# A second buffer for copied sums, a new order on VectorE, and the differences of xin stored in pairs

## The reference

```python
def _L0_cond_ref(x, c, weight, c_weight, bias):
    ...
    out = lax.conv_general_dilated(x, weight, window_strides=(STRIDE,), padding=[(PAD, PAD)], dimension_numbers=('NCH', 'OIH', 'NCH'), feature_group_count=GROUPS)
    ctx = jnp.einsum('nd,od->no', c, c_weight)
    out = out + ctx[:, :, None] + bias[None, :, None]
    return out

def _L1_cond_ref(x, embedding, W0, b0, W1, b1, W2, b2, weight, bias_k):
    ...
    att = jax.nn.softmax((h @ W2 + b2) / T, axis=-1)
    agg_w = jnp.einsum('bk,koi->boi', att, weight[..., 0])
    agg_b = att @ bias_k
    out = jnp.einsum('boi,bih->boh', agg_w, x) + agg_b[:, :, None]
    return out
...
x = x + _L0_cond_ref(x, cond_128, L0_cond_weight, L0_cond_c_weight, fside_S_0)
x = x + _L1_cond_ref(x, cond_128, L1_cond_W0, ...)
x = x + _L2_cond_ref(x, cond_128, L2_cond_weight, L2_cond_c_weight, fside_S_0)
x = x + _L3_cond_ref(x, cond_128, L3_cond_W0, ...)
```

## Time and profile before

| | us |
|---|---|
| median of 3 runs | 2769.24 (2769.07 to 2769.81) |
| the profiled execution's time | 2770.05 |
| its span in the trace | 2768.2 |
| TensorE matmul busy | 2622.8 (95%) |
| VectorE busy | 2150.6 (78%) |
| ScalarE busy | 1492.8 (54%) |

### The profile page before, as it was taken

How to read it: one execution, slowest core, us unless ns; L and a number is a source line. 1 busy time by engine, 2 the same in 40 slices (tenths; PEclk the granted TensorE clock), 3 DMA queues, 4 the chain that set the end, 5 groups by cost and what they waited for, 6 DMA issues and landing times.

```text
span 2768.2 us, 57051 instructions
## 1 busy us (share of the span) xinstructions
PE 2622.8 (95%) x24812; PEld 1174.4 (42%) x24812; DVE 2150.6 (78%) x815; ACT 1492.8 (54%) x852; POOL 36.7 (1%) x31
## 2 busy tenths in 40 slices
PE   6699999999999999999999999999999999999998
PEld 3244444444444444444444444444444444444443
DVE  4578788788788787787887887887887887878873
ACT  2345555555555555555555555555555555555554
POOL 5000000000000000000000000000000000000000
PEclk8699999999999999999999999999999999999999
DMA  5634434334334334334334334334434444443433
GB/s 155 212 131 142 122 114 146 119 114 150 115 114 152 114 114 152 114 114 152 114 115 150 114 121 144 121 121 136 129 121 129 132 126 122 139 123 117 144 92 107
DMA packets 185494, 357.06 MB, mean 129 GB/s; under 512 B 12715, under 2 KB 143795, under 8 KB 152635
## 3 DMA queue, kind: packets, MB, share of 16 engines
q1 hardware_dynamic: 184576, 352.37, 40.6%
q10 hardware_dynamic: 898, 4.39, 0.6%
HBM read 205.72 MB, written 150.99 MB: 129 GB/s over the span
## 4 chain that ended last, share of the span: by engine, by line
PE 66%; DVE 23%; issue 5%; ACT 5%; DMA 2%; DVEq 0%; ACTq 0%; SPq 0%
PE psum L313 25%; PE psum L325 22%; PE psum L350 17%; DVE diff L546 17%; DVE y L602 5%; ACT y L475 4%; DMA mix_dram<-y 1%; DVEq L137 0%; DVE y L595 0%; ACT y L464 0%; DMA select_sb<-select 0%; PE psum L274 0%; PE psum L303 0%; DMA mixw<-mix_dram 0%; ACT x L515 0%
## 5 line engine op out<-in xcount | busy, mean ns | idle before, releaser
L313 PE MATMUL psum<-diff,prod_w 32*128 32x512 f32 x8192 | 932.1, 596 | 89.0 <-DVE diff L546 69.6
L546 DVE TENSOR_TENSOR diff<-xin 128x2052 f32<-128x2052 f32 x256 | 984.4, 3890 | 0.0
L350 PE MATMUL psum<-y,mixw 32*128 32x512 f32 x8192 | 917.2, 595 | 20.2 <-DMA mixw<-mix_dram 13.7
L325 PE MATMUL psum<-diff,prod_w 32*128 32x512 f32 (+1 forms) x8192 | 773.2, 600 | 0.0
L472 ACT COPY shared<-psum 128x2048 f32<-128x2048 f32 x256 | 477.8, 1866 | 493.8 <-PE psum L313 493.8
L602 DVE TENSOR_TENSOR y<-y,shared 128x2048 f32<-128x2048 f32 x128 | 293.4, 2292 | 542.5 <-ACT y L475 542.5
L313 PEld LDWEIGHTS psum<-diff,prod_w 32*128 32x128 f32 x8192 | 414.9, 185 | 594.6 <-issue 410.6
L350 PEld LDWEIGHTS psum<-y,mixw 32*128 32x128 f32 x8192 | 418.5, 186 | 503.3 <-issue 497.6
L475 ACT COPY y<-psum 128x2048 f32<-128x2048 f32 x256 | 477.8, 1867 | 273.0 <-PE psum L325 273.0
L546 DVE TENSOR_TENSOR diff<-x 128x2055 f32<-128x2055 f32 x256 | 576.5, 2295 | 9.6 <-ACT x L515 9.6
L325 PEld LDWEIGHTS psum<-diff,prod_w 32*128 32x128 f32 (+1 forms) x8192 | 314.4, 158 | 435.8 <-issue 419.2
(11 more groups left out here) (57 smaller groups left out, 91.7 us busy)
## 6 DMA issues: line engine op xcount, KB each, us to landing
xin<-x SPq DMA_DIRECT2D x128, 1024.0 KB, 6.6
out<-outb SPq DMA_DIRECT2D x128, 1024.0 KB, 4.7
mixw<-mix_dram SPq DMA_DIRECT2D x512, 128.0 KB, 5.2
mix_dram<-y SPq DMA_DIRECT2D x16, 1024.0 KB, 4.5
y<-experts ACTq DMA_DIRECT2D x2, 512.0 KB, 12.6
x<-conv_w ACTq DMA_DIRECT2D x1, 768.0 KB, 9.6
shared<-conv_w ACTq DMA_DIRECT2D x1, 768.0 KB, 11.0
diff<-expert_rows ACTq DMA_DIRECT2D x4, 144.0 KB
```

The lines of the kernel that those rows point to most:

```text
L313: mm = pe.matmul(psum[:, half, g, :], prod_w[v][at, kind, s, :], diff[at, s, :, 0:R], start=first and s == 0, stop=last and s == PH - 1, s ...
L325: return pe.matmul(psum[cols, half, g, :], prod_w[v][at, kind, s, cols], diff[at, s, :, 0:R], start=False, stop=stop, skip_group_check=True)
L350: mm = pe.matmul(psum[:, half, r, :], mixw[m][at, b, g, :], y[m][at, :, g, b, :], start=g == 0, stop=g == GROUPS - 1)
L546: nc.vector.tensor_tensor(into(kind), in0, in1, op).then_inc(diff_ready[v], 1)
```

## The change

Three edits. First, the buffer shared becomes two, one for each convolution, and ScalarE waits before it overwrites one for VectorE's last use of that one (`y_ready[v]`), no longer for the other convolution's. Second, VectorE's order in a step: all four differences of x2 come first, then `outputs(0, i)`, then all four differences of the next xin, and `outputs(1, i-1)` last. With that come waits for the slots of diff0: ONLY_EVEN and ONLY_ODD of x2 for the front's BOTH and SIGNED products, BOTH and SIGNED of xin for the middle's two outer products. Third, the differences of xin are stored as pairs of neighbouring time steps: the operation reads two neighbouring elements, skips to the next block and so on, its result is contiguous as before, and the front's matmuls (not the middle's) read every other element of it, 8 bytes apart.

```diff
-        shared = sb("shared", [P, 2, GROUPS, BANK])
+        shared = [sb(f"shared{v}", [P, 2, GROUPS, BANK]) for v in range(2)]
...
+            def moving(v, kind, s):
+
+                diff = diff_of(v, kind)
+                if v == 1:
+                    return diff.rearrange("p (s b m) -> p s b m", s=PH, b=PB)[:, s]
+                return diff.rearrange("p (u b m w) -> p u w b m", u=2, w=2, b=PB)[:, s // 2, s % 2]
+
             def product(v, kind, half, first, last):
-                diff = diff_of(v, kind).rearrange("p (s b m) -> p s b m", s=PH, b=PB)
                 for s in range(PH):
                     for g in range(GROUPS):
                         at = slice(CG * g, CG * (g + 1))
-                        mm = pe.matmul(psum[:, half, g, :], prod_w[v][at, kind, s, :], diff[at, s, :, 0:R],
+                        mm = pe.matmul(psum[:, half, g, :], prod_w[v][at, kind, s, :], moving(v, kind, s)[at, :, 0:R],
...
-            def take_sums(v, n, earlier):
-
-                if earlier is not None:
-                    act.wait_ge(y_ready[1 - v], 2 * earlier + 2)
+            def take_sums(v, n):
                 for j, half in enumerate((A, B_HALF)):
                     act.wait_ge(conv_done[v], PRODUCTS * n + 1 + j)
-                    nc.scalar.copy(shared[:, j], psum[:, half, :, :]).then_inc(shared_ready[v], 1)
+                    if not (whole(n) and n == 0):
+                        act.wait_ge(y_ready[v], 2 * n)
+                    nc.scalar.copy(shared[v][:, j], psum[:, half, :, :]).then_inc(shared_ready[v], 1)
...
-                eighths = xin[:].rearrange("p (m c) -> p c m", c=BLOCK)
-                at = [eighths[:, PH * (q % 2):PH * (q % 2 + 1), q // 2:q // 2 + T - 1] for q in range(4)]
+                pairs = xin[:].rearrange("p (m j u w) -> p j u m w", j=PAR, u=2, w=2)
+                at = [pairs[:, q % 2, :, q // 2:q // 2 + T - 1] for q in range(4)]
                 make_diffs(0, at, kinds, lambda kind: diff_of(0, kind).rearrange(
-                    "p (s c) -> p s c", s=PH)[:, :, 0:T - 1])
+                    "p (u m w) -> p u m w", u=2, w=2)[:, :, 0:T - 1])
...
             def step(i):
                 if has_middle(i):
+                    diff_of_x2(i - 1, (BOTH, SIGNED))
                     if has_front(i):
-                        diff_of_x2(i - 1, (BOTH, SIGNED))
-                    else:
-                        diff_of_x2(i - 1, (BOTH, SIGNED, ONLY_EVEN, ONLY_ODD))
+                        dve.wait_ge(conv_done[0], PRODUCTS * i + 1)
+                    diff_of_x2(i - 1, (ONLY_EVEN,))
+                    if has_front(i):
+                        dve.wait_ge(conv_done[0], PRODUCTS * i + 2)
+                    diff_of_x2(i - 1, (ONLY_ODD,))
                 if has_front(i):
                     outputs(0, i)
                 if whole(i) and i <= 1:
                     stage_agg(i)
-                if has_middle(i) and has_front(i):
-                    dve.wait_ge(conv_done[0], PRODUCTS * i + 2)
-                    diff_of_x2(i - 1, (ONLY_EVEN, ONLY_ODD))
                 if has_next(i):
                     dve.wait_ge(conv_done[0], PRODUCTS * i + 4)
                     diff_of_xin(i + 1, (ONLY_EVEN, ONLY_ODD))
+                    if has_middle(i):
+                        dve.wait_ge(conv_done[1], PRODUCTS * i - 1)
+                    diff_of_xin(i + 1, (BOTH,))
+                    if has_middle(i):
+                        dve.wait_ge(conv_done[1], PRODUCTS * i)
+                    diff_of_xin(i + 1, (SIGNED,))
                 if has_middle(i):
                     outputs(1, i - 1)
-                if has_next(i):
-                    if has_middle(i):
-                        dve.wait_ge(conv_done[1], PRODUCTS * i)
-                    diff_of_xin(i + 1, (BOTH, SIGNED))
```

More of the change, by code:

```diff
@@ L74, in conditioned_layers @@
         scaled = [early[:, 2 + m].rearrange("p (k b) -> p k b", k=EXPERTS) for m in range(2)]
-        taps = [x2[:, 0:3 * BANK], shared[:].rearrange("p n g c -> p (n g c)")[:, 0:3 * BANK]]
+        taps = [x2[:, 0:3 * BANK], shared[1][:].rearrange("p n g c -> p (n g c)")[:, 0:3 * BANK]]
         taps = [t.rearrange("p (d s c) -> p d s c", d=3, s=PH) for t in taps]
@@ L317, in outer_products, with one_set @@
             def outer_products(v, n):
-                even = diff_of(v, ONLY_EVEN).rearrange("p (s b m) -> p s b m", s=PH, b=PB)
-                odd = diff_of(v, ONLY_ODD).rearrange("p (s b m) -> p s b m", s=PH, b=PB)
                 lower, upper = slice(0, P // 2), slice(P // 2, P)
-                def one_set(kind, diff, half, s, cols, g, stop):
+                def one_set(kind, half, s, cols, g, stop):
                     at = slice(CG * g, CG * (g + 1))
-                    return pe.matmul(psum[cols, half, g, :], prod_w[v][at, kind, s, cols], diff[at, s, :, 0:R],
+                    return pe.matmul(psum[cols, half, g, :], prod_w[v][at, kind, s, cols], moving(v, kind, s)[at, :, 0:R],
                                      start=False, stop=stop, skip_group_check=True)
@@ L330, in outer_products @@
                     for g in range(GROUPS):
-                        one_set(ONLY_EVEN, even, A, s, slice(0, P), g, False)
+                        one_set(ONLY_EVEN, A, s, slice(0, P), g, False)
                 for s in (0, 1):
                     for g in range(GROUPS):
-                        mm = one_set(ONLY_EVEN, even, A, s, lower, g, s == 1)
+                        mm = one_set(ONLY_EVEN, A, s, lower, g, s == 1)
                     if s == 0:
@@ L339, in outer_products @@
                     for g in range(GROUPS):
-                        one_set(ONLY_ODD, odd, B_HALF, s + 2, upper, g, False)
+                        one_set(ONLY_ODD, B_HALF, s + 2, upper, g, False)
                 for s in (0, 1):
                     for g in range(GROUPS):
-                        mm = one_set(ONLY_ODD, odd, B_HALF, s, slice(0, P), g, s == 1)
+                        mm = one_set(ONLY_ODD, B_HALF, s, slice(0, P), g, s == 1)
                 mm.then_inc(conv_done[v], 1)
@@ L489, in step @@
                         act.wait_ge(taps_ready, 2)
-                    take_sums(0, i, None if whole(i) and i < 2 else i - 2)
+                    take_sums(0, i)
                 if whole(i) and i <= 1:
@@ L506, in step @@
                             act.wait_ge(agg_stored[j], 16 * SETS)
-                    take_sums(1, i - 1, i if has_front(i) else None)
+                    take_sums(1, i - 1)
                 if has_front(i):
@@ L598, in outputs @@
                 flat = y[v][:].rearrange("p j g b m -> p j (g b m)")
-                kept = shared[:].rearrange("p j g c -> p j (g c)")
+                kept = shared[v][:].rearrange("p j g c -> p j (g c)")
                 dve.wait_ge(shared_ready[v], 2 * n + 2)
```

## The result

The changed kernel takes 2686.54 us (median of 4 runs, 2685.1 to 2687.56) against 2769.52 us for the kernel before in the same comparison (4 runs, 2769.07 to 2770.21): ratio 0.970, 95% interval 0.9683 to 0.9717. That is 83 us less, and 26.5 us more than the forecast of 2660. The wide range, 2655 to 2700, holds it; the forecast's own range, 2655 to 2670, does not.

The account below looks back on a forecast made before the run. TensorE was taken as the bound, stalled at 62 fronts by VectorE's late differences: 2770.05 - 103.5 (stalls) - 5.5 (opening) = 2661.0 us profiled, so 2660 predicted; own range 2655 to 2670, wide range to 2700.

Parts of the forecast that it names:

- The wide range: Whole kernel: 2655 to 2700 us, to hold 8 in 10, reaching to the partial cases.
- the forecast's own range: Whole kernel: 2655 to 2670 us if the main forecast, chance 0.75, holds.
- What bounds the kernel: Front of each step: TensorE waits for VectorE's xin differences, queued behind `outputs(1, i-1)`; 1.67 us lost in each step.
- 62 x 1.67 = 103.5 us: Loop: 62 late fronts each lose 1.67 us, a period of 41.27 us against 39.60 back to back.
- The order alone removes the whole stall: VectorE's queue: with the new order differences are ready before the front even at 3.88 us each; gain 103.5 us.
- In the steady state it makes no difference to the sum: VectorE's xin differences in the loop: pairs take 2.30 us, not 3.88, but off the path, so no gain.
- I take 0: TensorE's front matmuls and outer products: reading every other element, 8 bytes apart, costs 0; from above, ratio 1.69.
- the partial rival: Front: part of the stall remains or TensorE loses a few per cent; 2712 or 2701 us; chance 0.14.
- its second cause: TensorE's front: matmuls five per cent slower, giving 2701 us.
- The rule of the Trainium skill: Reads of pairs: at least two hits per 16-byte line hide memory latency; cited for VectorE's 2.30 us and against slower TensorE.
- The opening, 5.5 us: Ahead of step 0: three shorter xin differences start the first front 4.75 us earlier; 5.5 us taken, between 0 and 7.9.

Follow-up runs that it names:

- the first experiment: The changed kernel with the differences of xin in the old layout, so two shared buffers and the new order alone: 2659.78 us, ratio 0.9604 against the kernel before.
- the second: The kernel before, its own order and one shared buffer, with only the pairs added: 2685.96 us, ratio 0.970 against the kernel before.
- the last experiment: The new order with the old layout, and pairs for the first pair of sequences alone: 2654.82 us, ratio 0.9585 against the kernel before.

## Why the prediction was right in kind and 26 us off in size

- **What bounds the kernel.** Right. The stall at the front hung on the place of its differences behind `outputs(1, i-1)`; moving them, or making them shorter, removed all 62.
- **"62 x 1.67 = 103.5 us."** Undersized. The period without a stall is 39.48 us (the new order alone), so each stall was 1.79 us and the term is 62 x 1.79 = 111 us. I had given the first mix the 7.06 us of the last mix; it takes 6.95. The chain leaves TensorE just there, so it did not show this mix, and I filled in its neighbour.
- **"The order alone removes the whole stall."** Right, shown by the first experiment, and by the one with one shared buffer for the order without the second buffer, which the prediction had called needed as spare time. But so do the pairs alone, by the second; the edits are two cures for one wait, and I did not work out the second in the prediction.
- **"In the steady state it makes no difference to the sum"**, said of VectorE's part of the pairs: right. 1.58 us less for each difference only became idle time.
- **The step that failed: "I take 0"** for TensorE's 8-byte steps. It is 0.52 us a step (13.25 instead of 12.73), 4.1% of 12.73, 33 us over 64 fronts. This is the partial rival (chance 0.14), by its second cause. My argument compared bytes walked per ns and took the limit from VectorE's 32-byte jumps, 16.9. Up to steps of 16 bytes TensorE's limit is 16 / 1.76 = 9.1 bytes per ns, and the pairs ask it for 9.5. Nor are bytes walked the measure beyond 16 bytes, as the 32-byte step shows. It is the number of 16-byte pieces touched: 1.76 ns each on TensorE. Two elements from each piece arrive every 0.88 ns, and TensorE at its upper clock level wants one every 430 / 512 = 0.84 ns. VectorE takes 2.30 us for 2052 contiguous elements, one every 1.12 ns with its start included, or 2.24 ns for a pair, and a jump costs it 1.89 ns (3.88 us for 2052), so for it the same pairs are fast enough.
- **The rule of the Trainium skill** (Advanced Engine Details and Errata, SBUF Cachelines) that at least two hits on a 16-byte line are needed to hide the memory's latency was my second support; I read it as saying that two are enough. Read so, the front would have kept its 12.73 us; the trace has 13.25, so for TensorE reading fp32 the measurement decides against that reading, by 5% of a matmul. For VectorE the rule and the trace agree, 2.30 us.
- **The opening, 5.5 us.** Right in size: 5.0 us in the last experiment by the medians and 3.6 by the traces, with one front's 0.52 us already paid. The three differences beside GpSimd took 8.10 us, 2.70 on the mean, as estimated. Of the clock, part came back: the first front's 64 instructions took 9.11 us instead of 10.00, though they read pairs. A part of it went again, as later groups of the opening ran at a lower clock: the first mix of step 0 took 9.80 us at a granted clock of 0.72, against 8.94 us at 0.79 in the new order alone.
- **Luck.** The undersized stall (7.5 us too little) and the surplus that was put at nothing (33 us) have opposite signs. Had the stall been sized right, the forecast would have been about 2652, and the miss 34 us.

Put together with the measured terms: 2770.05 - 111 - 5 + 33 = 2687 (2688 with the 3.6 us of the traces for the opening), against 2687.56 for the profiled execution of the changed kernel. The new order alone differs from the changed kernel by 26.8 us: 33.3 for the fronts, less 5.0 for the opening, less 1.7 for a mix in step 64, which takes 8.85 us there, at a granted clock of 0.65 and 0.62 in its first 4.7 us, and 7.15 in the changed kernel, at 1.00. In both TensorE had been idle for 2.09 us before it. That last piece is read from the two traces and was not tried by itself; why the clock fell in one of them stays open.

## What to carry to other kernels

An operand's layout has a writer and a reader, and here one of them was the bottleneck. Pairs made VectorE's operation 1.58 us shorter 256 times where it had time to spare, and TensorE's instructions 4% longer where it had none; the order, at no price, gave all the gain of the loop. Use a layout that suits the idle engine only where that engine is on the path, here once, before the first front. And when two edits are made for the same wait, work out each alone: the sum of their gains isn't to be had.

## What the runs showed of the hardware

- TensorE, fp32, 512 columns, four matmuls of 32 rows side by side: 430 ns contiguous, 450 ns at 8-byte steps, 675 at 12, 900 at 16, 918 at 32. At the upper clock level and up to 16 bytes this is the greater of 430 ns and 1.76 ns for each new 16 bytes. The 16-byte steps take 900 ns at the lower clock level too.
- At the lower clock level (granted clock 0.50 from 36.9 to 39.4 us) the 8-byte steps cost nothing, as the 450 ns for the pieces are less than the 850 ns that contiguous reads take there. The first front's weight loads in the changed kernel follow each other every 0.85 us at first, like those of contiguous reads in the kernel before, and later every 0.45 us:

```profile
37.73 0.36 PEld L319 LDWEIGHTS psum<-diff,prod_w 32*128 32x128 f32 x4 [0.49 <-issue]
38.59 0.36 PEld L319 LDWEIGHTS psum<-diff,prod_w 32*128 32x128 f32 x4 [0.49 <-issue]
...
41.14 0.20 PEld L319 LDWEIGHTS psum<-diff,prod_w 32*128 32x128 f32 x4 [0.25 <-issue]
41.59 0.20 PEld L319 LDWEIGHTS psum<-diff,prod_w 32*128 32x128 f32 x4 [0.25 <-issue]
```

- VectorE's TENSOR_TENSOR of 2052 fp32 elements: 2.30 us with pairs read and contiguous writes, 3.88 with reads at 32-byte steps, and 3.89 with pairs read and writes that alternate between two places 2 KB apart.
